# Moving spike arithmetic and last products around the final two FFN groups of a one-core gated block

## The reference

```python
# x is (8, 224, 512); z = layernorm(x)
h = square(relu(z @ W_fc.T))         # 2048 wide
y = h @ W_proj.T                     # 512 wide
mem = 0
for step in range(5):
    reset = mem > 1
    mem = 0.9 * mem + y - reset
    spk = mem > 1
    total += spk
x = x + tanh(g_ffn) * total / 5
```

## Time and profile before

| | |
|---|---|
| median of 3 runs | 1140.63 us (1138.51 to 1142.62) |
| profiled execution, its own time | 1138.57 us |
| its span in the trace | 1136.7 us |
| TensorE busy | 1078.6 us (95%) |
| VectorE busy | 753.7 us (66%) |
| ScalarE busy | 572.5 us (50%) |
| group 2, TensorE's loop begins | about 968.5 us |
| group 3, TensorE's loop begins | about 1016.3 us |

### The profile page before, as it was taken

One profiled execution on the slowest core, in us unless ns is written; L12 is line 12 of the kernel. 1 busy time (PEld: TensorE's weight loads), 2 busy tenths in 40 slices (PEclk: granted clock), 3 DMA queues, 4 the chain that ended last, 5 costly groups with the idle time before them and its releaser, 6 DMA issues.

```text
span 1136.7 us, 19369 instructions
## 1 busy us (share of the span) xinstructions
PE 1078.6 (95%) x7165; PEld 886.8 (78%) x7165; DVE 753.7 (66%) x1168; ACT 572.5 (50%) x1082; POOL 289.1 (25%) x265
## 2 busy tenths in 40 slices
PE   2999999999999999999999999997999999998984
PEld 2987877877887887887788787775888888996773
DVE  4247777786787686787787687777432654655767
ACT  4345845754764664655565484553545333453400
POOL 1003343353343423532543344322000000000000
PEclk9789999999999999999999999998999999999997
DMA  5300201101100010020120200132420002001111
GB/s 163 112 32 1 72 2 33 62 9 32 43 27 25 21 57 8 24 70 0 32 70 0 69 0 0 33 84 74 156 74 19 1 1 89 24 1 38 38 37 38
DMA packets 31337, 47.45 MB, mean 42 GB/s; under 512 B 2241, under 2 KB 10449, under 8 KB 31297
## 3 DMA queue, kind: packets, MB, share of 16 engines
q1 hardware_dynamic: 31296, 46.91, 12.9%
HBM read 39.56 MB, written 7.34 MB: 41 GB/s over the span
## 4 chain that ended last, share of the span: by engine, by line
PE 90%; DVE 6%; issue 1%; DMA 1%; SPq 1%; ACT 1%; DVEq 0%; ACTq 0%
PE work L413 51%; PE score L734 12%; PE heads_out L533 8%; PE score L496 8%; PE score L428 2%; PE maxes L666 2%; PE maxes L518 1%; PE heads_out L545 1%; PE maxes L508 1%; DVE spikes L1495 1%; DMA xin<-in_x 1%; DVE neuron L1499 1%; DVE neuron L1497 1%; PE score L413 1%; SPq L304 1%
## 5 line engine op out<-in xcount | busy, mean ns | idle before, releaser
L1603 POOL TENSOR_TENSOR dsum<-dsum,probs 125x448 f32<-125x448 f32 x186 | 225.2, 1211 | 14.6
L413 PE MATMUL work<-xT,wk 128*128 128x488 f32 (+1 forms) x768 | 187.2, 395 | 0.0
L413 PE MATMUL work<-wv,xT 128*125 128x512 f32 (+1 forms) x768 | 187.2, 397 | 0.0
L413 PE MATMUL work<-zT,wf 128*128 128x512 f32 (+1 forms) x768 | 165.6, 366 | 1.0 <-issue 1.0
L413 PEld LDWEIGHTS work<-wv,xT 128*125 128x125 f32 (+1 forms) x768 | 137.8, 183 | 36.8 <-issue 2.3
L413 PEld LDWEIGHTS work<-xT,wk 128*128 128x128 f32 x768 | 142.1, 191 | 31.0 <-issue 4.6
L865 ACT ACTIVATE probs<-score 125x448 f32<-125x448 f32 (+1 forms) x256 | 119.9, 550 | 76.3 <-PE score L496 75.9
L413 PEld LDWEIGHTS work<-zT,wf 128*128 128x128 f32 x768 | 132.7, 190 | 24.1 <-issue 1.4
L1600 POOL TENSOR_TENSOR dsum<-probs 125x448 f32<-125x448 f32 x31 | 36.4, 1173 | 445.6 <-ACT probs L871 445.6
L1207 DVE TENSOR_TENSOR probs<-probs,maxes 125x1792 f32<-125x1792 f32 x64 | 128.3, 2015 | 6.4 <-PE maxes L518 5.9
L734 PE MATMUL score<-hT,wp 128*128 128x512 f32 (+1 forms) x576 | 117.7, 354 | 0.0
(11 more groups left out here) (158 smaller groups left out, 1430.6 us busy)
## 6 DMA issues: line engine op xcount, KB each, us to landing
xin<-in_ctx SPq DMA_DIRECT2D x48, 250.0 KB
neuron<-in_L_ffn_W_fc SPq DMA_DIRECT2D x16, 256.0 KB, 4.5
neuron<-in_L_ffn_W_proj SPq DMA_DIRECT2D x16, 256.0 KB, 2.7
xin<-in_x SPq DMA_DIRECT2D x16, 224.0 KB, 9.7
xres<-in_x SPq DMA_DIRECT2D x16, 224.0 KB, 2.7
x_scratch<-xres SPq DMA_DIRECT2D x16, 224.0 KB, 2.3
out<-fin SPq DMA_DIRECT2D x14, 256.0 KB, 2.1
zt<-x_scratch SPq DMA_DIRECT2D x3, 1024.0 KB, 5.6
```

The source lines that it names most:

```text
L413: mm = pe.matmul(bank, lhs(i, k), rhs(j, k), start=(n == 0), stop=(n == len(passes) * chunks - 1))
L1603: pool.tensor_tensor(total[0:ROWS[t]], total[0:ROWS[t]], tile(t), ALU.add).then_inc(dchain if t < TILES - 1 else dsum_done, 1)
```

## The change

Three things move; no instruction is added or taken away.

1. Group 1's neuron steps 19 to 25 move out of VectorE's loop of group 3 into its loop of group 2, where the last seven values of j now carry two steps instead of one. In group 3, `finish(1, ...)` stands at j = 1 and 4 (before: 5 and 6), group 2's steps at j = 4 to 12 (before: 6 to 13). `finish(2, 0, 1)` keeps its place at j = 14.
2. On TensorE the `spikes_back` calls of group 1 stand at j = 2 and 4 (before: 4 and 5), that of group 2 at j = 15 (before: 14).
3. The last two products of chunk 0 come after two and five products of chunk 1 (before: after four and eight). `unit_back(0)` comes after five products of chunk 2 (before: after two). `unit_back(1)` is issued inside the first `last_down`, behind j = 6 (before: behind its end).

```diff
-            def last_down(at, n, bank):
+            def last_down(at, n, bank, back=None):
...
-                mm.then_inc(y_mm, 1)
+                    if j == FC - 1:
+                        mm.then_inc(y_mm, 1)
+                    if j == 6 and back is not None:
+                        unit_back(back)
...
# TensorE, final_group
                     up(3, j)
                     if j >= 2:
                         down(3, j - 2, (0,))
+                    if j == 2:
+                        spikes_back(1, 0, 1)
                     if j == 4:
-                        spikes_back(1, 0, 1)
-                    if j == 5:
                         spikes_back(1, 2, 3)
-                    if j == 14:
+                    if j == 15:
                         spikes_back(2, 0, 1)
-                for j in range(4):
+                for j in range(FC):
                     down(3, j, (1,))
-                down(3, FC - 2, (0,))
-                for j in range(4, 8):
-                    down(3, j, (1,))
-                down(3, FC - 1, (0,))
-                for j in range(8, FC):
-                    down(3, j, (1,))
+                    if j == 1:
+                        down(3, FC - 2, (0,))
+                    if j == 4:
+                        down(3, FC - 1, (0,))
                 for j in range(FC):
                     down(3, j, (2,))
-                    if j == 1:
+                    if j == 4:
                         unit_back(0)
-                last_down(0, TG // 2, 3)
-                unit_back(1)
+                last_down(0, TG // 2, 3, 1)
                 last_down(TG // 2, TG // 2, 0)
...
# VectorE, third_group (group 2)
                     else:
-                        neuron_steps(1, 12 + (j - 9), 12 + (j - 8))
+                        neuron_steps(1, 12 + 2 * (j - 9), 12 + 2 * (j - 8))
                 group_lo(3, *range(NT[3]))
...
# VectorE, final_group (group 3)
                     h_lo_part(3, j)
-                    if j < 4:
-                        n = 19 + 7 * j // 4
-                        neuron_steps(1, n, 19 + 7 * (j + 1) // 4)
-                    if j in (5, 6):
-                        finish(1, 2 * j - 10, 2 * j - 9)
-                    if 6 <= j < 14:
-                        neuron_steps(2, 26 * (j - 6) // 8, 26 * (j - 5) // 8)
+                    if j in (1, 4):
+                        finish(1, *((0, 1) if j == 1 else (2, 3)))
+                    if 4 <= j < 13:
+                        neuron_steps(2, max(3 * j - 13, 0), 3 * j - 10)
                     if j == 14:
                         finish(2, 0, 1)
```

## The result

The changed kernel takes 1127.99 us in the median of four runs (1126.34 to 1129.12), the kernel before 1141.38 us (1138.51 to 1142.62, four runs with one more than before the prediction). The ratio is 0.9885 with a 95% interval of 0.9862 to 0.9908: faster by 1.2%. The forecast was 1128.1 us.

What follows compares the result with a forecast made beforehand. TensorE bounds the kernel up to about 1016 us, then TensorE and VectorE alternate, and from about 1086 us almost only VectorE. 7.0 - 1.2 + 2.0 + 4.6 = 12.4, taken as 12.5: 1140.63 - 12.5 = 1128.1 us, range 1124.2 to 1131.8.

Steps and rivals of the forecast that it cites:

- Step 1: Group 2's loop on VectorE: seven more neuron steps make group_lo(3) late and TensorE wait, a loss of 1.2 us.
- The rule of the Trainium skill that spoke against it: VectorE in group 2's loop: next operation waits until the pipe has emptied, period 2.95 us, group_lo(3) about 1.3 us later.
- rival C: VectorE before group 3: its instructions don't overlap when packed, 1.3 us more, 1129.4 us; chance 0.04.
- Step 2: Group 3's loop on TensorE: no gap left, 55.2 us instead of 62.3, a gain of 7.0 us.
- Step 3: Behind group 3's loop: chunk 0's end seven products after the loop, not ten, a gain of 2.04 us.
- Step 4: Tail: VectorE's stalls of 2.51 us for chunk 2 and 2.11 us for unit 1's transposes go, a gain of 4.6 us.
- The cover at chunk 2: Tail, before unit 2: VectorE may start at 1097.1 and gets there at 1097.4, only 0.4 us of cover.
- A: TensorE's new gap before group 3 also costs clock, everything behind it 1.6 us later, 1129.7 us; chance 0.10.
- B: Tail: the 0.4 us of cover at unit 2 doesn't hold, some 1 us of stall stays, 1129.1 us; chance 0.12.
- D: Whole kernel: the change does nothing that can be measured, 1140 us; chance 0.02.
- E: TensorE after the gap before group 3: the low clock stays, slower, 1144 us at 16 us of it; chance 0.02.

Runs made afterwards that it cites:

- run with `group_lo` first: Changed kernel with the last two neuron steps of group 1 behind group_lo(3) on VectorE, not ahead of it: 1127.05 us in the median, ratio 0.9881.
- one of 2.21 us in the same place: Changed kernel with two further VectorE instructions (bn_stats) ahead of group_lo(3): 110.1 us from group 3's token transposes to the end, changed kernel 109.0.
- the run with 2.80: Changed kernel with three further VectorE instructions (bn_stats) ahead of group_lo(3): 112.3 us from group 3's token transposes to the end, changed kernel 109.0.

## Why the prediction was right

**Step 1, the hand-over.** Predicted: periods of 2.74 us, `group_lo` from 1015.0 to 1017.5, a loss of 1.2. With the 2.0 us taken off, it ran from 1014.98 to 1017.46, and TensorE started at 1017.51 instead of 1016.34, 1.17 later. The run with `group_lo` first shows the cause by taking it away. The rule of the Trainium skill that spoke against it (VectorE: DVE Perf Modes, "The DRAIN you can't avoid") would, by an estimate, make the period at least 0.42 + 1.22 + 1.22 = 2.86; the rows give 2.72 to 2.74. The prediction's 2.95 rests on small gaps for which it names no row, and at 2.86 VectorE would still have kept up with 2.88, so rival C's 1.3 us was too much. The same section says that a next operation that isn't held starts earlier, and that is what these rows look like; I had used its first sentence alone.

**Step 2, group 3's loop.** Predicted 55.2 us, measured 54.9 (1019.51 to the end of the last transposes at 1074.44 on the chain). So the gain was 7.3 rather than 7.0, and 7.5 if the loop of before is counted from TensorE's start at 1016.34 too, as the 1.17 of step 1 is. Two terms were mis-sized. I took 0.62 us for eight transposes, from a place where TensorE had just waited. Without a wait they take 0.46 (chain of waits, after):

```profile
1028.66 0.24 PE maxes L767 x4
1028.89 0.22 PE heads_out L767 x4
```

Three times 0.16 is 0.5 us, and nothing follows the third eight inside the loop, another 0.1. The first 36 matmuls, behind their wait, took 8.46 us where the sum has 3 x 2.72 = 8.16: that takes 0.3 back. `finish(1, 0, 1)` waited for the transposes as foreseen and ended at 1028.4 in the old clock of times, against 1028.3 predicted.

**Step 3.** Unit 0's first step came 66.36 us after the transposes' start, before 74.63: 8.3 us sooner, where 7.9 were predicted. The 0.4 comes from step 2. The residual's transfer was issued at 1077.84, 14 us before its first use.

**Step 4.** From unit 0's first step to `finish_unit(1)` it was 26.91 us before, 22.35 after: 4.56, predicted 4.6. `unit_back(0)` went out at 1090.02 without a wait. The cover at chunk 2 was 0.54 us, predicted 0.4. The runs with each `unit_back` at its old place show that both new places count. Their prices, 0.8 and 1.7 us with chunk 0 sooner, are not the two stalls of before (2.51 and 2.11) one by one.

**The rivals.** A: the gap came out at 1.02 us and cost no clock, nor did one of 2.21 us in the same place; the run with 2.80 shows that the mechanism is real. B: the cover held, by half a microsecond. C: fell by the 2.74. D and E: did not occur. The forecast of the median rested on 1140.63 for the kernel before; the later 1141.38 makes the measured gain 13.4 us in medians, of which 12.8 are seen in the trace and the rest is within the spread of runs. So the forecast's 1128.1 lies only 0.1 us from the measured 1127.99 by luck: the sum was 0.3 us short by the trace, and the runs of either kernel spread by 3 to 4 us. The lower bound of the range also took 2.7 us for the spread of runs where the runs give 2.1; nothing hung on it.

## What to carry to other kernels

An idle gap on the engine that is the bound is worth more than its length once it is long enough to cost clock (here gaps of 2.74 us and more did, and cost some 1.6 us each; gaps up to 2.21 didn't); look at whether the consumer of a buffer stands behind an instruction that the waiting engine itself has just fed, and move the consumer a loop step ahead. Filling idle time with moved work is free only while something is left to absorb the other delays of that stretch: here 0.14 us of slack in a period of 2.88 turned one late input into 1.2 us at the next hand-over, and putting the hand-over's own work in front took it away. In a tail where one engine's serial chain sets the end, feed it sooner only as far as the second input allows, and move every instruction that was timed against the first with it.

## What the runs showed that I had not expected

**Where executions part.** Twelve profiled executions of twelve kernels, whose code is the same up to group 2, start group 3's token transposes anywhere from 1011.7 to 1016.6 us. Most of it is there by 100 us, where the twelve lie from 0.2 us ahead of the kernel before to 4.2 behind it, and they keep that distance to 720 us. Between 760 and 820 us eleven of them shift against it once more, by 0.8 us one way to 0.7 the other, and then not again up to 960. Where the record gives a granted clock of 0.76 to 0.78 for the stretch from 24 to 50 us (four of the twelve, the kernel before among them) the start is at 1011.7 to 1012.2 us; where it gives 0.98 or 1.00 (the other eight), at 1013.6 to 1016.6. At the same time the 48 matmuls of two columns at 25 us take 7.66 to 8.68 us in the former and 10.40 in the latter (TensorE, before and after):

```profile
25.27 8.44 PE L666 MATMUL maxes<-shift_in,wk 128*128 128x2 f32 x48 [1.07 <-DVE wk L1414]
```

```profile
25.10 10.40 PE L666 MATMUL maxes<-shift_in,wk 128*128 128x2 f32 x48 [0.84 <-DVE wk L1414]
```

That the stretch recorded at the higher clock is the slower one doesn't fit together; it may be that the record has no low level where the execution began in it. What sets it was not tried and stays open. So 4.4 us of spread stand at 720 us, ahead of the feed-forward part, where no edit in it can touch them, and this is why the distances above are counted from a common point.

**The clock's answer to gaps at one place.** Behind 1.02 and 2.21 us of idle time the granted clock was 1.00; behind 2.80 us it was 0.67, and 1.62 us were lost.
